# First group's preparation in a fused rotation, attention and quantized-FFN kernel: work moved between VectorE, ScalarE and GpSimd

## The reference

```
a = amplitudes ** delta_t;  ang = frequencies * delta_t       # per sequence (64) and channel pair
c, s = a * cos(ang), a * sin(ang)
x0, x1 = the two halves of the rotated axis of x
rotated = [c * x0 - s * x1,  s * x0 + c * x1]

q, k, v = rotated @ W_qkv.T, 16 heads of 16
k = layernorm(k) over the 16 numbers of a head
gamma = sigmoid(log_gamma)                                    # one decay rate per head
S_t = gamma * S_{t-1} + v_t k_t^T;  y_t = S_t q_t;  x = x + y @ W_o.T

x = x + ffn(pooled attention over the 64 tokens of a sequence)   # gate, up, down; fake quantized
```

## Time and profile before

| | |
|---|---|
| device time, three runs | 279.13 us median (278.16 to 279.15) |
| profiled execution | 279.3 us, span 277.6 us |
| PE busy | 255.3 us (92%) |
| DVE busy | 232.6 us (84%) |
| ACT busy | 180.6 us (65%) |
| POOL busy | 145.2 us (52%) |

### The profile page before, as it was taken

One profiled execution on the slowest core, in us unless ns is written; L12 is line 12 of the kernel. 1 busy time (PEld: TensorE's weight loads), 2 busy tenths in 40 slices (PEclk: granted clock), 3 DMA queues, 4 the chain that ended last, 5 costly groups with the idle time before them and its releaser, 6 DMA issues.

```text
span 277.6 us, 8491 instructions
## 1 busy us (share of the span) xinstructions
PE 255.3 (92%) x3545; PEld 176.0 (63%) x3545; DVE 232.6 (84%) x501; ACT 180.6 (65%) x316; POOL 145.2 (52%) x140
## 2 busy tenths in 40 slices
PE   5898999988998899899899999998889999998995
PEld 5767769657877777777777886885634434433331
DVE  4999869479699878978987786787888999999994
ACT  2775481552467647768748547527689999847991
POOL 6939595990593278059339533003212679850570
PEclk9999999999999999999999999999999999999999
DMA  5990504400900530194084033040009489000167
GB/s 164 336 275 3 153 0 151 159 2 13 293 5 2 190 117 2 35 291 43 0 302 62 2 129 84 2 138 22 0 0 200 113 219 348 35 0 0 72 256 280
DMA packets 30311, 31.20 MB, mean 112 GB/s; under 512 B 12929, under 2 KB 20673, under 8 KB 30273
## 3 DMA queue, kind: packets, MB, share of 16 engines
q1 hardware_dynamic: 30272, 30.66, 37.2%
HBM read 19.48 MB, written 8.42 MB: 100 GB/s over the span
## 4 chain that ended last, share of the span: by engine, by line
PE 45%; DVE 32%; ACT 13%; issue 6%; DMA 1%; POOL 1%; DVEq 0%; ACTq 0%
PE psum L879 11%; PE psum L1271 6%; PE psum L904 4%; DVE yT_lo L1480 4%; PE psum L1290 3%; DVE psum L1475 3%; PE psum L986 3%; ACT silu L842 2%; PE psum L961 2%; ACT silu L824 2%; PE psum L1030 2%; DVE arena L1468 2%; PE psum L942 2%; PE psum L1023 2%; DVE arena L1651 2%
## 5 line engine op out<-in xcount | busy, mean ns | idle before, releaser
L1460 DVE TENSOR_TENSOR arena<-psum,xq_mem 128x512 f32<-128x512 f32 x64 | 39.7, 682 | 7.0 <-PE psum L904 7.0
L531 POOL TENSOR_TENSOR xT_lo<-arena,xT 128x512 fp32r<-128x512 f32 x14 | 18.0, 1308 | 46.1 <-ACT xT L662 46.1
L1271 PE MATMUL psum<-xq_mem,guT 128*128 128x512 bf16 x152 | 33.9, 380 | 0.2
L662 ACT ACTIVATE xT<-arena 128x512 fp32r<-128x512 f32 x14 | 8.1, 623 | 29.5 <-PE psum L879 26.0
L1271 PEld LDWEIGHTS psum<-xq_mem,guT 128*128 128x128 bf16 x152 | 14.4, 98 | 19.4 <-DVE arena L1651 1.8
L1662 DVE TENSOR_REDUCE h_max<-arena 128x1 f32<-128x1024 f32 (+1 forms) x24 | 25.9, 1123 | 0.2
L824 ACT ACTIVATE silu<-psum,gu_x 128x1024 f32<-128x1024 f32 (+1 forms) x24 | 24.4, 1025 | 2.1 <-PE psum L1271 1.1
L879 PE MATMUL psum<-wT,xT 128*128 128x256 f32 x64 | 17.3, 293 | 4.8 <-DVE arena L1468 4.8
L1475 DVE SCALAR_TENSOR_TENSOR psum<-psum,pmask,arena 128x256 f32<-128x256 f32 x28 | 12.3, 485 | 10.0 <-ACT arena L651 10.0
L904 PE MATMUL psum<-arena 32*64 32x128 f32 x1024 | 19.3, 278 | 1.1 <-issue 1.1
L644 ACT ACTIVATE arena<-psum,pmask 128x512 f32<-128x512 f32 x32 | 20.1, 684 | 0.1
(11 more groups left out here) (251 smaller groups left out, 734.1 us busy)
## 6 DMA issues: line engine op xcount, KB each, us to landing
arena<-in_x SPq DMA_DIRECT2D x9, 512.0 KB, 3.8
x_dram<-arena SPq DMA_DIRECT2D x8, 512.0 KB, 4.1
pooled<-x_dram SPq DMA_DIRECT2D x8, 512.0 KB, 5.3
out<-pooled SPq DMA_DIRECT2D x15, 256.0 KB, 2.2
xin<-in_x_t SPq DMA_DIRECT2D x7, 512.0 KB, 4.5
cs_rows<-cs_dram SPq DMA_DIRECT2D x12, 256.0 KB, 5.2
pooled<-in_w_qkv_t SPq DMA_DIRECT2D x3, 256.0 KB, 4.9
pooled<-in_w_down SPq DMA_DIRECT2D x1, 704.0 KB, 7.4
```

The lines of the kernel that those rows point to most:

```text
L531: pool.tensor_tensor(xT_lo[:, k, :], xrotT[:, k, :], xT[:, k, :].bitcast(F32), ALU.subtract).then_inc(xl_ok, 1)
L1271: mm = pe.matmul(in_order(o[:, 512 * half:512 * half + 512], 2 * n + half), gT[i][:, v, c, :], xq_rows(2 * n + half, c), start=(c == 0), s ...
L1460: dve.tensor_tensor(dec[:, c, r, :, :], bank[S_BANK[r]].rearrange("q (n k) -> q n k", n=PP), two_heads, ALU.mult).then_inc(dec_done, 1)
```

## The change

The logarithm of the decay rates moves to the head of ScalarE's queue, ahead of the sines, and is made there alone (absolute value, exp, ln with bias 1). The rotation of the first group is split: ScalarE multiplies by the sine (8 instructions of 128x128), VectorE does the rest (8 fused instructions of 128x128). GpSimd centres the K weights and makes the high part of the Q weights, sets `steps` above the diagonal to 1e20, so that the decay arguments are two plain 128x512 products, and takes its triangle selections and powers in another order. Its `rotate(1)` no longer waits for `dec_arg`. ScalarE's exponential of the decays is split in two and interleaved with the Q copies. TensorE does the first Q half ahead of turning all of `cs`, and has 2 dummy products where 10 stood. Some semaphores are merged.

```diff
@@ gpsimd
+            bounds(0)                        # three selections on base[0:64]
             pool.wait_ge(ld_cols, 16)
             pool.wait_ge(ang_ok, 1)
-            for part in (slice(0, 2 * PP), slice(2 * PP, NPAIR)):
-                n = part.stop - part.start
-                pool.tensor_tensor(a_pow[:, part], a_col.to_broadcast([P, n]), dt_b[:, part], ALU.pow).then_inc(pow_ok, 1)
+            powers(slice(0, 2 * PP))
+            pool.wait_ge(pow_ok, 1)
+            for b in range(2):
+                half = slice(S * b, S * b + S)
+                pool.affine_select(out=steps[half, :], in_=steps[half, :], compare_op=ALU.is_ge, fill=FAR, base=0,
+                                   pattern=[[1, S]], channel_multiplier=-1).then_inc(lg_ok, 1)
+                pool.wait_ge(lg_ok, b + 1)
+            pool.wait_ge(ld_k, 16)
+            pool.wait_ge(mean_ok, 1)
+            pool.tensor_tensor(centred.rearrange("p c (h d) -> p c h d", d=DK), raw_qkv[:, :, D:2 * D].rearrange("p c (h d) -> p c h d", d=DK),
+                               mean[:, :, :].unsqueeze(3).to_broadcast([P, DC, NH, DK]), ALU.subtract).then_inc(centred_ok, 1)
+            pool.wait_ge(ld_q, 16)
+            pool.tensor_copy(wT[:, 0, :, :], raw_qkv[:, :, 0:D]).then_inc(wqv_ok, 1)
+            pool.wait_ge(ld_v, 16)
+            pool.tensor_copy(wT[:, 2, :, :], raw_qkv[:, :, 2 * D:3 * D]).then_inc(wqv_ok, 1)
+            powers(slice(2 * PP, NPAIR))
...
                 if g == 1:
                     pool.wait_ge(csr_ok, 2)
-                    pool.wait_ge(dec_arg, 1)
...
+            pool.wait_ge(pow_ok, 2)
+            bounds(1)                        # three selections on base[64:128]
             pool.tensor_tensor(base[:, 3, :], base[:, 0, :], base[:, 2, :], ALU.subtract).then_inc(base_ok, 1)
             pool.tensor_tensor(base[:, 4, :], base[:, 1, :], base[:, 2, :], ALU.subtract).then_inc(base_ok, 1)
-            pool.wait_ge(ld_v, 16)
-            pool.tensor_copy(wT[:, 2, :, :], raw_qkv[:, :, 2 * D:3 * D]).then_inc(wv_ok, 1)
             rotate(1)
@@ scalar
+            act.wait_ge(ld_row, 16)
+            link(act.activation(lg[:, 1, :], lg_raw, ACT.Abs))
+            link(act.activation(lg[:, 2, :], lg[:, 1, :], ACT.Exp, scale=-1.0))
+            act.activation(lg[:, 3, :], lg[:, 2, :], ACT.Ln, bias=1.0).then_inc(lg_ln, 1)
             act.wait_ge(ang_ok, 2)
             act.activation(ang[:, 4, :], ang[:, 2, :], ACT.Sin).then_inc(trig_ok, 1)
             act.activation(ang[:, 5, :], ang[:, 3, :], ACT.Sin).then_inc(trig_ok, 1)
-            act.wait_ge(ld_q, 16)
-            act.activation(wT[:, 0, :, :], raw_qkv[:, :, 0:D], ACT.Copy).then_inc(w_ok, 1)
-            act.wait_ge(lg_abs, 2)
-            act.activation(lg[:, 2, :], lg[:, 1, :], ACT.Exp, scale=-1.0).then_inc(lg_exp, 1)
+            act.wait_ge(x0_in, 16)
+            act.wait_ge(cs1_ok, 1)
+            for h in range(2):
+                other = x1[1][:, :, HW:D] if h == 0 else x1[1][:, :, 0:HW]
+                for n in range(PP):
+                    act.activation(rot[:, h, n, :], other[:, n, :], ACT.Identity, scale=cs[:, 1, n:n + 1]).then_inc(rot_part, 1)
...
             act.wait_ge(cs_tr, 1)
             act.activation(cs_T[:, :], bank[4][0:2 * NPAIR, 0:P], ACT.Copy).then_inc(csT_ok, 1)
-            act.wait_ge(dec_arg, 1)
-            act.activation(decay, decay, ACT.Exp).then_inc(dec_exp, 1)
-            q_copies(0, 0)
-            q_copies(0, 1)
+            for c in range(DC):
+                q_copies(0, c)
+                act.wait_ge(dec_arg, c + 1)
+                act.activation(decay[:, HC * c:HC * c + HC, :], decay[:, HC * c:HC * c + HC, :], ACT.Exp).then_inc(dec_exp, 1)
@@ tensor
-            keep_clock(2, bank[3][:, 0:P], ident[:, :], ident[:, :])
...
-                keep_clock(4, bank[3][:, 0:P], ident[:, :], ident[:, :])
+                keep_clock(1, bank[3][:, 0:P], ident[:, :], ident[:, :])
...
+            pe.wait_ge(wl_ok, 1)
+            project_x(0, Q_BANK, 0, 0, q_mm)
             pe.wait_ge(cs_ok, 2)
             pe.wait_ge(csr_ok, 2)
             pe.transpose(bank[4][0:2 * NPAIR, 0:P], cs[:, :, :].rearrange("p k n -> p (k n)"), ident[:, :]).then_inc(cs_tr, 1)
-            pe.wait_ge(wl_ok, 1)
-            project_x(0, Q_BANK, 0, 0, q_mm)
             squares(0, 0)
@@ vector
-            dve.tensor_scalar(lg[:, 4, :], lg_raw, -1.0, None, ALU.mult).then_inc(lg_abs, 1)
-            dve.tensor_tensor(lg[:, 1, :], lg[:, 4, :], lg_raw, ALU.max).then_inc(lg_abs, 1)
...
             dve.wait_ge(pow_ok, 1)
             dve.wait_ge(trig_ok, 2)
-            dve.tensor_tensor(cs[:, 0, first], a_pow[:, first], ang[:, 5, first], ALU.mult)
-            dve.tensor_tensor(cs[:, 1, first], a_pow[:, first], ang[:, 4, first], ALU.mult).then_inc(cs1_ok, 1)
+            dve.tensor_tensor(cs[:, 1, first], a_pow[:, first], ang[:, 4, first], ALU.mult)
+            dve.tensor_tensor(cs[:, 0, first], a_pow[:, first], ang[:, 5, first], ALU.mult).then_inc(cs1_ok, 1)
...
-            (six 128x512 instructions of the rotation, L1391 to L1401, and the centring, L1407)
+            for h, (sign, half) in enumerate(((ALU.subtract, rot_left), (ALU.add, rot_done))):
+                cols = slice(HW * h, HW * h + HW)
+                for n in range(PP):
+                    dve.wait_ge(rot_part, PP * h + n + 1)
+                    last = dve.scalar_tensor_tensor(xrot[:, n, cols], x1[1][:, n, cols], cs[:, 0, n:n + 1], rot[:, h, n, :], ALU.mult, sign)
+                last.then_inc(half, 1)
+            dve.wait_ge(centred_ok, 1)
             dve.tensor_copy(wT[:, 1, :, :], centred).then_inc(wk_ok, 1)
...
             low_weights(0, raw_qkv[:, :, 0:D], wT[:, 0, :, :], wT_lo[:, 0, :, :])
+            dve.wait_ge(lg_ln, 1)
+            link(dve.scalar_tensor_tensor(lg[:, 4, :], lg_raw, 0.0, lg[:, 3, :], ALU.min, ALU.subtract))
+            link(dve.tensor_scalar(lg[:, 4, :], lg[:, 4, :], LEAST, None, ALU.min))
+            dve.wait_ge(lg_ok, 2)
+            for c in range(DC):
+                heads = slice(HC * c, HC * c + HC)
+                dve.tensor_tensor(decay[:, heads, :], steps[:, :].unsqueeze(1).to_broadcast([P, HC, S]),
+                                  lg[:, 4, heads].unsqueeze(2).to_broadcast([P, HC, S]), ALU.mult).then_inc(dec_arg, 1)
+            low_weights(1, raw_qkv[:, :, 2 * D:3 * D], wT[:, 2, :, :], wT_lo[:, 2, :, :])
             dve.wait_ge(pow_ok, 2)
             (the other 24 columns of cosine and sine, unchanged)
-            for h in range(NH):
-                last = dve.scalar_tensor_tensor(decay[:, h, :], steps[:, :], lg[:, 4, h:h + 1], later[:, :], ALU.mult, ALU.add)
-            last.then_inc(dec_arg, 1)
             sums_copy(0)
-            low_weights(1, raw_qkv[:, :, 2 * D:3 * D], wT[:, 2, :, :], wT_lo[:, 2, :, :])
```

## The result

The median of 20 runs is 278.15 us, against 279.74 us for 20 runs of the kernel before: a ratio of 0.9942 (95% 0.9927 to 0.9957), 0.6% faster. I had forecast 280.9 and slower. The profiled execution has a span of 276.5 us (277.6 before). The order of events is the one that the first rival describes. That the median also meets its time of 278.3 is partly luck: its gain of 0.6 to 1.0 was counted from 279.13, and the measured gain is 1.1 in the span and 1.6 in the medians.

What follows compares the result with a forecast made beforehand. The bound was the wait chain to TensorE's first values. 17.95, + 0.5 (differences), + 2.4 (`rotate(1)` turns) gave X = 20.8; + 11.1 ended `decays(0, 1)` at 31.9 against 30.07: 1.8 us slower, 280.9, range 276.5 to 282.3.

Steps and rivals of the forecast that it cites:

- the first rival: First GpSimd selection falls behind VectorE's low Q weights, `rotate(1)` after `cs_ok`: 0.6 to 1.0 us faster, 278.3; chance 0.18.
- X: End of VectorE's second product of 24 columns (`cs_ok` 2); forecast 20.8, with `decays(0, 1)` ending 11.1 later.
- My even point: The end of VectorE's second 24-column product, 18.97, at which `decays(0, 1)` would end at 30.07 as before.
- The first selection fits in at 14.5, before VectorE's low Q weights begin (14.76): GpSimd after its second power: its first triangle selection goes ahead of VectorE's low Q weights.
- my lead of 0.25: Margin by which GpSimd's first selection was to precede VectorE's low Q weights; said to decide the order.
- The term of 2.4: Two instructions of GpSimd's `rotate(1)` take turns ahead of VectorE's two products of 24 columns, adding 2.4 us.
- The centring 7.65 to 8.93: GpSimd's centring of the K weights, its duration bounded by the 1.27 to 1.29 of other 128x512 instructions.
- GpSimd's Q copy takes its turn, 0.61, to 9.6; second product and `cs1_ok` at 9.7: Behind the centring, the Q copy delays VectorE's second 128x8 product; `cs1_ok` at 9.7 instead of 8.13.
- 9.48 less 0.26: From `newton(0)` to the end of `decays(0, 1)`, less the wait for TensorE; taken as 9.15 us.
- The third rival: Centring does not hold up VectorE's 128x8 products: `decays(0, 1)` ends at 27.65, 2.4 us faster, 276.7; chance 0.20.
- 0.83 ns a column: ScalarE's rotation products: cost per column, giving 0.39 us for a 128x128 product, one every 0.285.
- The sines' 7.74: ScalarE's front: with separate table loads for exp and ln, the sines end at 7.74 instead of 7.13.

Runs made afterwards that it cites:

- e1: Changed kernel with the centring of the K weights back on VectorE, directly behind the mean; 278.3 and 278.8 us, no ratio.
- e2: Changed kernel with GpSimd's two differences on `base` moved behind `rotate(1)`, so that `rotate(1)` begins earlier; 283.72 us, ratio 1.012.
- e3: Changed kernel with the decay arguments as sixteen 128x64 instructions again instead of two products; 290.13 us, ratio 1.036.
- e8: Changed kernel with the ten dummy products of the kernel before instead of two; 278.51 us, ratio 0.994.
- e9: Changed kernel with GpSimd's centring waiting for VectorE's first products of cosine and sine (`cs1_ok`); 278.06 us, ratio 0.992.
- e11: Changed kernel with `rotate(1)` waiting for the decay arguments (`dec_arg` 2) again; 277.86 us, ratio 0.989.
- e4: Kernel before with only the decay arguments made as two products, GpSimd setting `steps` above the diagonal; 278.82 us, ratio 0.996.
- e5: Changed kernel with the differences on `base` behind `rotate(1)`, and `rotate(1)` also waiting for `cs_ok` 2; 278.09 us, ratio 0.992.
- e7: Changed kernel with the edits of e1, e5 and e6 together; 276.76 us, ratio 0.985.
- e10: e7 with GpSimd's Q copy also waiting for the first products of cosine and sine (`cs1_ok`); 276.89 us, ratio 0.985.
- e6: Changed kernel with TensorE's sums of squares ahead of the turn of `cs`; 277.30 us, ratio 0.990.

## Why the prediction was wrong

**The mechanism held in the main.** VectorE's instructions with two SBUF inputs and GpSimd's large ones hold each other up for whole instructions: 0.95 for 128x8 behind the centring, 0.70 for a selection behind the low Q weights, 1.24 for a product of 24 columns behind a rotation product (e1, e2), 9.49 for the sixteen (e3). With one input it can happen too (1.27 for `kind` 128x32 in e2, 0.17 in the changed kernel). The sum from X on held where TensorE kept its clock: `newton` at X + 1.95 (1.96 measured) and the end at X + 11.1 (10.97, and 10.98 in e1; 12.05 and 12.33 in e2 and e3). My even point, X = 18.97, is borne out by both sides: X = 18.40 (e1) was faster at that stage and 19.38 (e2) slower.

**The step that failed** is "The first selection fits in at 14.5, before VectorE's low Q weights begin (14.76)". Both engines came earlier than I had them, and VectorE by more. The low Q weights began at 14.12 (0.64 earlier), the first selection at 14.21 (some 0.3 earlier), so my lead of 0.25 became a lag of 0.09. `rotate(1)` was to start at 18.15 in front of the products, and started at 17.39 at their end; X was to be 20.8 and was 17.56. The difference of 3.2 adds up: 0.64 from the earlier start, 0.25 because the two differences cost VectorE 0.25 and not 0.5, and 2.4 for the two turns of `rotate(1)`, which cost nothing. The first rival names this condition, with X = 17.9 to 18.4; that X came out below its bounds is the 0.64.

**The term of 2.4 was not borne out either, even with the forecast's order.** In e1 the first selection had its lead, and `rotate(1)` cost one turn, not two: X = 18.40. The prediction took it that the one that waits gets its turn between any two instructions of the other. Three times a small product that started in the same hundredth as GpSimd's next instruction went through in 0.15 to 0.17 (8.78 and 17.39 in the changed kernel, 18.23 in e1). By what rule the two take turns then is open.

**Two terms upstream were mis-sized, and they moved the order:**

- "The centring 7.65 to 8.93": 7.78 to 8.84. 1.06 instead of 1.28, whose bounds I had taken from products of two full inputs; here one is the mean, 32 wide and repeated. As it also started later, it ended only 0.1 earlier.
- "GpSimd's Q copy takes its turn, 0.61, to 9.6; second product and `cs1_ok` at 9.7": the second product ran in 0.15 at 8.78, at the same time as the Q copy, and `cs1_ok` came at 8.93. This is 0.8 of VectorE's lead, of which the rotation kept 0.55 (done at 11.95 instead of 12.5). GpSimd was freed by only 0.36 (power at 9.94 instead of 10.3).

The first alone would have moved both engines about alike; the second moved VectorE by more. What I should have weighed is that a lead of 0.25 rested on two chains of seven or more terms each, so the order was close to open. I gave the forecast twice the chance of the rival. The edge is not at zero, though, and the measured order is not as close to flipping as 0.09 sounds. In e8 the first selection started 0.01 ahead of the low Q weights and still waited (0.80), and in e9 it came 0.61 behind them and `rotate(1)` started at 17.43.

**Slips in the working that did not decide.** 9.48 less 0.26 is 9.22, not 9.15. The third rival's 27.65 should be 27.5 (16.4 + 11.1). The 0.83 ns a column of ScalarE's product is not in the rows named: 0.62 for 512 columns and 1.137 for 1024 give 1.0 ns, and by that a product would take 0.23; that it took 0.385, as forecast, is luck as far as those rows go. And L1386, called an instruction "without GpSimd beside" it, ran beside the power, as the prediction says itself further on.

**What was right.** The sines' 7.74 (7.80 measured), with separate loads for exp and ln. Here the Trainium skill, "ScalarE: Activation LUTs", section "Table sets: the hidden batching unit", would have one load for both; no run here has it, and the row at 4.64, a load between exp and ln, stands against it. ScalarE's products every 0.285 us (2.45 for eight, predicted 0.39 + 7 x 0.285 = 2.39). That the rotation ends about where it did: 12.5 predicted, 11.95 measured, 12.11 before. From `cs1_ok` to its end it takes 3.02 instead of 3.98, and `cs1_ok` comes 0.80 later (8.93 instead of 8.13), so nearly all that ScalarE's help saves is lost ahead of it. The dummies and the removed wait cost nothing that can be measured (e8, e11); the earlier Q half was not tried by itself. Of the third rival, the looser lock, only a piece is there (the Q copy beside the second product), and e9 shows that freeing both products wins nothing.

**Where the gain came from.** 1.54 at the end of `decays(0, 1)`: in the kernel before, two products for sixteen arguments give 0.75 (e4, shown). The parts don't simply add up: with the rest of the change in place, the sixteen cost 9.20 there (e3), because `rotate(1)` now runs among them. The other 0.8 is what the centring off VectorE, the earlier rotation and TensorE's new order make together. Only parts of it are shown. With the centring back on VectorE the end was 0.85 later (e1), but by the turn of `rotate(1)`. Where the wait keeps that out in both kernels, X is 17.27 with the centring on GpSimd (e5) and 17.08 with it on VectorE (e7, which differs besides only in TensorE's squares). So the centring on GpSimd is no gain by itself; it pays here because it makes GpSimd late enough for `rotate(1)` to come last. How the rest divides between the rotation and TensorE's order stays open. That 0.4 is given back later is read from the profile; which wait takes all of it was not tried.

## What to carry to other kernels

Where two engines share a path by whole instructions, the order of their turns decides more than the work saved: a shift of 0.4 us between the two queues was worth 0.84 us at X (e1), and one instruction group in another place 1.8 us at X and 5.5 in the span (e2). Where a forecast rests on such an order, give both orders nearly equal chances, or better, fix it with a wait on the critical instruction's semaphore (e5 and e7: one wait, no cost). At a contested moment, few large instructions in the queue that must get through are safer than many small ones (e3).

## What the runs showed of the chip that I had not expected

- A GpSimd copy is not always in the way. In the changed kernel the Q copy and the second 128x8 product both start at 8.78 and take 0.63 and 0.15; in e1 a copy that started at 7.60 beside VectorE's centring took 1.13 and held the first product from 8.18 to 8.75. Copies beside the fused instructions made them longer (2.54 in e10 against e7's 2.28, 2.67 in e6 against 2.36).
- TensorE's granted clock fell to 0.5, its level of 1.2 GHz, where it had little or nothing to do first: 0.57 us of work in 18 to 20 (e2, then 0.64 and 0.51) and none in 18 to 24 (e3: 0.55 in the last two of these, 0.50 behind them). My expectations priced a late X by its delay alone and were short by 2 to 3 us in both; 1.1 (e2) and 1.4 (e3) of that lie between X and the end of `decays(0, 1)`, beside the low clock. In the changed kernel the clock is 1.00 over the whole profiled execution.
- A 128x512 subtraction on GpSimd took 1.06 with one input a repeated 32 columns, against 1.27 to 1.30 with two full ones.
